# Two-layer transformer kernel: a bridge phase before the linear-attention stack, with changes to the first loads, the slot marks and the closing mixture

## What is computed

```python
def reference(...):
    # layer 0
    x = x + ga * L0_attn(layernorm(x) * (1 + ca) + sa)      # 16 heads of 64, causal, softmax
    x = x + gb * L0_ffn(layernorm(x) * (1 + cb) + sb)       # 8 experts, each takes its 512 best tokens
    # layer 1, with its own sa, ca, ga, sb, cb, gb
    x = x + ga * L1_attn(layernorm(x) * (1 + ca) + sa)      # a stack of 8 linear-attention layers
    x = x + gb * L1_ffn(layernorm(x) * (1 + cb) + sb)       # top 2 of 8 linear experts
    return x

def L0_ffn(x):          # the experts' part
    probs = softmax(rmsnorm(x) * norm_weight @ router_w.T + router_b)
    gates, idx = top_k(probs.T, 512)
    ye = gelu(xn[idx] @ fc1.T + b1) @ fc2.T + b2            # per expert
    out = zeros.at[idx].add(ye * gates);  return out / sum_of_gates_per_token

def L1_attn(x):         # 8 times
    Q = elu(x @ Wq + bq) + 1;  K = elu(x @ Wk + bk) + 1;  V = x @ Wv + bv
    att = Q * sum(K * V) / (Q * sum(K) + 1e-6)              # sums over a sequence
    x = norm(gelu(att @ Wo + bo) + x);  x = norm(gelu(gelu(x @ W1 + b1) @ W2 + b2) + x)

def L1_ffn(x):
    gates = top2(softmax(x @ Wg)), made to sum to 1
    return sum(gates[e] * (x @ We[e] + be[e]))
```

## Time and profile before

| | us |
|---|---|
| median of 3 runs | 3410.51 (3409.53 to 3415.76) |
| the profiled execution | 3412.19 |
| its span | 3410.5 |
| mean granted clock of TensorE | 0.949 |
| setup and loads | 0 to 15.9 |
| attention | 15.9 to 570 |
| router | 570 to 609 |
| choice of tokens and experts | 609 to 806 |
| combine | 806.4 to 824.4 |
| clearing of 114 semaphores | 824.4 to 832.8 |
| stack entry | 833.1 to 853.8 |
| stack up to its first matmul with weights | 854 to 874 |
| stack | 874 to 3247 |
| tail | 3247 to 3403 |
| clearing of 93 semaphores | 3403 to 3410 |

### The profile page before, as it was taken

How to read it: one execution, slowest core, us unless ns; L and a number is a source line. 1 busy time by engine, 2 the same in 40 slices (tenths; PEclk the granted TensorE clock), 3 DMA queues, 4 the chain that set the end, 5 groups by cost and what they waited for, 6 DMA issues and landing times. The chain is left out here.

```text
span 3410.5 us, 52149 instructions
## 1 busy us (share of the span) xinstructions
PE 3024.9 (89%) x14384; PEld 1972.1 (58%) x14384; DVE 2768.5 (81%) x10994; ACT 2423.9 (71%) x4513; POOL 558.3 (16%) x663
## 2 busy tenths in 40 slices
PE   6999998272599999999999999999999999999678
PEld 5777776161456565565656656656565666666342
DVE  5878786853489998988998999899899989988454
ACT  5888886031488887887887888888788888888420
POOL 0000001383101111111111111111111211211110
PEclk9999998595799999999999999999999999999869
DMA  1000000322100000000000000000000000000000
GB/s 53 1 1 1 1 0 10 103 34 36 54 1 1 5 28 2 1 7 27 1 7 26 1 3 30 2 1 7 26 1 7 26 2 2 15 1 1 0 4 22
DMA packets 35107, 46.95 MB, mean 14 GB/s; under 512 B 5704, under 2 KB 26240, under 8 KB 34816
## 3 DMA queue, kind: packets, MB, share of 16 engines
q1 hardware_dynamic: 29184, 39.47, 3.5%
q0 software_dynamic: 5632, 4.20, 0.9%
HBM read 35.16 MB, written 8.49 MB: 13 GB/s over the span
## 5 line engine op out<-in xcount | busy, mean ns | idle before, releaser
L1841 DVE TENSOR_SCALAR t_feat_q<-t_recip,t_neg_mean 128x256 f32<-128x256 f32 x1024 | 387.3, 440 | 132.7 <-ACT t_recip L1682 125.7
L1513 PE MATMUL t_o_ps<-t_feat_q,t_wo 128*128 128x512 f32 x1024 | 475.3, 597 | 13.7 <-issue 11.0
L1674 ACT ACTIVATE t_recip<-t_feat_q,t_z_scale 128x256 f32<-128x256 f32 x1024 | 434.8, 498 | 3.5 <-DVE t_feat_q L1841 2.7
L1660 ACT ACTIVATE t_exp_k<-t_k_ps 128x1024 f32<-128x1024 f32 x256 | 259.5, 1014 | 228.3 <-PE t_k_ps L1487 228.3
L1804 DVE CUSTOM_DVE_ANT_0 t_junk<-t_v_ps,t_feat_k 128x256 f32<-128x256 f32 x1024 | 390.5, 419 | 9.9 <-PE t_v_ps L1487 9.8
L1794 DVE SCALAR_TENSOR_TENSOR t_feat_k<-t_exp_k,t_k_ps 128x256 f32<-128x256 f32 x1024 | 369.0, 416 | 18.6 <-ACT t_exp_k L1660 18.5
L1664 ACT ACTIVATE t_exp_q<-t_q_ps 128x1024 f32<-128x1024 f32 x256 | 261.5, 1022 | 86.4 <-PE t_q_ps L1487 86.2
L1830 DVE SCALAR_TENSOR_TENSOR t_feat_q<-t_exp_q,t_q_ps 128x1024 f32<-128x1024 f32 x256 | 312.7, 1221 | 8.8
L1513 PEld LDWEIGHTS t_o_ps<-t_feat_q,t_wo 128*128 128x128 f32 x1024 | 194.3, 190 | 189.0 <-issue 168.9
L1972 POOL TENSOR_TENSOR t_var_eps<-t_moments,t_ln_eps 128x4 f32<-128x4 f32 x128 | 69.1, 540 | 1294.6 <-DVE t_moments L1852 1294.6
L1485 PE MATMUL t_v_ps<-t_x_hi,t_w_hi 128*128 128x512 f32 x512 | 265.3, 518 | 10.4 <-DVE t_sum_kv L1804 9.4
(11 more groups left out here) (351 smaller groups left out, 7211.4 us busy)
## 6 DMA issues: line engine op xcount, KB each, us to landing
t_raw_w<-in_wq SPq DMA_DIRECT2D x8, 512.0 KB, 4.0
t_raw_w<-in_wk SPq DMA_DIRECT2D x8, 512.0 KB, 4.6
t_raw_w<-in_wv SPq DMA_DIRECT2D x8, 512.0 KB, 6.1
t_wo<-in_wo SPq DMA_DIRECT2D x32, 128.0 KB, 2.3
x<-in_x SPq DMA_DIRECT2D x4, 512.0 KB, 7.0
tokens_dram<-r_hn SPq DMA_DIRECT2D x8, 256.0 KB, 2.3
e_w_raw<-in_fc_w SPq DMA_DIRECT2D x4, 512.0 KB, 4.0
e_w<-in_fc_w SPq DMA_DIRECT2D x4, 512.0 KB, 4.9
```

The costliest lines, as they stand in the source:

```text
L1513: last = pe.matmul(o_ps[:], wo[:, chunk, :], feat_q[:, s, chunk, :], start=(chunk == 0), stop=(chunk == NC - 1), skip_group_check=True)
L1660: act.activation(exp_k[:], k_ps[:], ACT.Exp, bias=-1.0).then_inc(c["k_exp"], 1)
L1674: last = act.activation(recip[:, q % 2, k * UNIT + n * SEQ:k * UNIT + (n + 1) * SEQ], feat_q[:, s, chunk, cols], ACT.Ln, bias=1.0, scale=z ...
L1841: last = dve.tensor_scalar(feat_q[:, s, chunk, cols], recip[:, q % 2, k * UNIT + n * SEQ:k * UNIT + (n + 1) * SEQ], -1.0, neg_mean[:, s, n ...
```

## The change

Four things are changed.

**1. First loads.** SP issues `w_q` and `w_kv` ahead of x and `w_o` behind it, in `setup_phase`. ACT rounds and DVE subtracts there too. In the attention phase SP raises `started` behind its 28 counters; the four other engines wait for it first.

The core of the diff:

```diff
 setup_phase, SP
+            sp.dma_start(g["w_raw"][:, 0, :], d["w_q"]).then_inc(g["w_in"][0], 16)
+            sp.dma_start(g["w_raw"][:, 1, :], d["w_kv"]).then_inc(g["w_in"][1], 16)
             for q in range(4):
                 sp.dma_start(g["x"][:, q * 8:q * 8 + 8, :], d["x"][:, q * 8:q * 8 + 8, :]).then_inc(x_in, 16)
+            sp.dma_start(g["w_o"][:], d["w_o"]).then_inc(g["w_o_in"], 16)
             sp.wait_ge(x_in, 64)
...
 causal_attention_phase, SP
             start_counters(sp, c.values())
-            sp.dma_start(w_raw[:, 0, :], d["w_q"]).then_inc(w_in, 16)
-            sp.dma_start(w_raw[:, 1, :], d["w_kv"]).then_inc(w_in, 16)
-            sp.dma_start(w_o[:], d["w_o"]).then_inc(w_in, 16)
-            sp.wait_ge(w_in, 48)
+            sp.sem_inc(started, 1)
+            sp.wait_ge(g["w_o_in"], 16)
...
 choose_and_run_experts_phase, ACT and DVE
+            act.activation(column_ps, column[:], ACT.Copy).then_inc(column_ready, 1)
...
-                dve.tensor_tensor(one_hot[e % 2][:], column[:].unsqueeze(1).broadcast_to([P, TILES, P]),
+                dve.tensor_tensor(one_hot[e % 2][:], column_ps.unsqueeze(1).broadcast_to([P, TILES, P]),
...
 bridge_phase, POOL
+            for k in range(TURNS + 1):
+                if k < TURNS:
+                    add_term(k)
+                if k >= 1:
+                    find_rstd(k - 1)
+                if k >= 3:
+                    split_low(2 * k - 6)
+                    split_low(2 * k - 5)
...
 bridge_phase, ACT
+            act.wait_ge(t["raw_w_in"], 49)
+            for n in range(TURNS):
+                if n < 6:
+                    round_high(2 * n)
+                    round_high(2 * n + 1)
+                modulate(n)
...
 bridge_phase, DVE
+            for k in range(TURNS + 2):
+                if k < TURNS:
+                    terms(k)
+                if 1 <= k <= TURNS:
+                    find_moments(k - 1)
+                if k >= 2:
+                    normalise(k - 2)
...
 tail_phase, POOL
+            for at in range(0, EXPERTS * TURNS, 2):
+                pool.wait_ge(c["hs_hi_ready"], at + 1)
+                if at >= RING:
+                    pool.wait_ge(c["hs_used"], at - RING + 1)
+                pool.tensor_tensor(hs_lo[:, at % RING, :], hs[:, at % RING, :], hs_hi[:, at % RING, :].bitcast(F32), ALU.subtract)\
+                    .then_inc(c["hs_lo_even"], 1)
...
 tail_phase, PE
             def expert(n, e):
                 at = EXPERTS * n + e
-                pe.wait_ge(c["hs_ready"], at + 1)
-                pe.matmul(sum_ps[n % 2][:], w_mix[:, e * D:(e + 1) * D], hs[:, at % RING, :], start=False, stop=(e == EXPERTS - 1),
+                cols = slice(e * D, (e + 1) * D)
+                pe.wait_ge(c["hs_hi_ready"], at + 1)
+                pe.matmul(sum_ps[n % 2][:], w_hi[:, cols], hs_hi[:, at % RING, :], start=False, stop=False, skip_group_check=True)
+                pe.matmul(sum_ps[n % 2][:], w_lo[:, cols], hs_hi[:, at % RING, :], start=False, stop=False, skip_group_check=True)
+                pe.wait_ge(c["hs_lo_odd"] if at % 2 else c["hs_lo_even"], at // 2 + 1)
+                pe.matmul(sum_ps[n % 2][:], w_hi[:, cols], hs_lo[:, at % RING, :], start=False, stop=(e == EXPERTS - 1),
                           skip_group_check=True).then_inc(c["hs_used"], 1)
```

More of the change, by code:

```diff
@@ L125, in _ @@
             act.activation(cond_e[:], cond[:], ACT.Exp, scale=-1.0).then_inc(exp_done, 1)
-            act.wait_ge(exp_done, 1)
+            for k in range(2):
+                act.wait_ge(g["w_in"][k], 16)
+                act.activation(g["w_hi"][:, k, :], g["w_raw"][:, k, :], ACT.Copy).then_inc(g["w_split_hi"], 1)
         @block.vector
@@ L258, in _ @@
         def _(act):
-            act.wait_ge(w_in, 48)
-            for k in range(2):
-                act.activation(w_hi[:, k, :], w_raw[:, k, :], ACT.Copy).then_inc(w_split_hi, 1)
+            act.wait_ge(started, 1)
             def drain_q(j, k):
@@ new lines, in find_moments, with normalise @@
+            def find_moments(n):
+                dve.wait_ge(c["x_added"], n + 1)
+                for i in range(GT * n, GT * n + GT):
+                    dve.bn_stats(stats[:, i, :], g["x"][:, i, :]).then_inc(c["bn_done"], 1)
+                dve.wait_ge(c["bn_done"], GT * n + GT)
+                for i in range(GT * n, GT * n + GT):
+                    dve.bn_aggr(moments[:, i, :], stats[:, i, :]).then_inc(c["stats_ready"], 1)
+            def normalise(n):
+                dve.wait_ge(c["rstd_ready"], n + 1)
+                if n >= 2:
+                    dve.wait_ge(c["x_turned"], n - 1)
+                for i in range(GT):
+                    tile = GT * n + i
+                    last = dve.tensor_scalar(xn[:, n % 2, i, :], g["x"][:, tile, :], moments[:, tile, 0:1], rstd[:, tile:tile + 1],
+                                             ALU.subtract, ALU.mult)
+                last.then_inc(c["xn_ready"], 1)
@@ L1287, in _ @@
+            for k in range(TURNS + 2):
[5 more added lines that the diff above has]
+                    normalise(k - 2)
         @block.tensor
         def _(pe):
+            pe.wait_ge(c["ones_made"], 1)
+            for q in range(QX):
+                pe.wait_ge(c["diag_ready"], 4 * q + 4)
+                pe.matmul(gate[q][:], ones[:], diag[:, 4 * q:4 * q + 4, :], start=True, stop=True).then_inc(c["gate_filled"], 1)
@@ L1689, in step @@
                     split_x(0, 0)
-                    for kind, q in SWAPS:
-                        swap(0, kind, q)
                 if Dn:
@@ L2133, in _ @@
             for n in range(TURNS):
-                if n + 1 < TURNS:
-                    copy_rows(n + 1)
-                gate_sums(n)
+                for e in range(EXPERTS):
+                    split_high(EXPERTS * n + e)
+                    if e == 0 and n + 1 < TURNS:
+                        copy_rows(n + 1)
+                    if e == 2 and n:
+                        gate_sums(n - 1)
+            gate_sums(TURNS - 1)
         @block.vector
@@ L2333, in _ @@
             LAST = EXPERTS * TURNS
-            for at in range(2):
+            pe.wait_ge(c["w_split"], 1)
+            for at in range(WIDE):
                 widen(at // EXPERTS, at % EXPERTS)
@@ L2396, in block0 @@
                 g["hn_stored"] = [sem(f"r_hn_stored{s}") for s in range(2)]
-                causal_attention_phase(nc, sem, d, g)
+                with ExitStack() as weights:
+                    held = lambda n, s, t=F32: weights.enter_context(nc.sbuf_tensor(n, s, t))
+                    g["w_raw"] = held("a_w_raw", [P, 2, CH])
+                    g["w_hi"] = held("a_w_hi", [P, 2, CH], F32R)
+                    g["w_lo"] = held("a_w_lo", [P, 2, CH], F32R)
+                    g["w_o"] = held("a_w_o", [P, NC, D])
+                    g["w_in"] = [sem(f"a_w_in{k}") for k in range(2)]
+                    g["w_o_in"], g["w_split_hi"], g["w_split_lo"] = (sem(n) for n in ("a_w_o_in", "a_w_split_hi", "a_w_split_lo"))
+                    setup_phase(nc, sem, d, g)
+                    causal_attention_phase(nc, sem, d, g)
                 g["route"] = local("route", [P, EXPERTS, TILES])
```

289 lines of the change are left out of this document (166 added, 123 removed), and 6 rows, old and new, of tables (STACK_COUNTERS, names).

## The result

The changed kernel took 3376.2 us in the median of 6 runs (3362.1 to 3388.9), the one before 3411.9 in as many. The ratio is 0.9902, 95% interval 0.988 to 0.9924, which is 33 us less. The forecast was 3367 with a range of 3352 to 3386: the time lies inside it, and above the forecast. The profiled execution took 3382.81 us, one of the slower of the six.

What follows compares the result with a forecast made beforehand. It asked which engine ends each touched phase, since each ends in a barrier: POOL in the experts, PE in the tail's loop. -7.5 - 15.5 - 12.9 + 1.4 - 8.9 = -43.4 off 3410.5 gave 3367.1, range 3352 to 3386.

Steps and rivals of the forecast that it cites:

- First loads: Kernel's start: weights loaded ahead of x and split under its load, first `bn_stats` at about 18.0, -7.5 us.
- Slot marks: Experts phase: a mark with one operand in PSUM no longer blocks POOL's gathers and scatters, -15.5 us.
- walk through the lists: Experts phase: stepping through the engines' operations in order, the phase's end comes 15.5 us earlier, last scatter about 774.
- a PSUM operand doesn't free POOL: Rival on the experts' marks: DVE work of that length blocks POOL anyway, marks gain nothing, 3383 us; chance 0.10.
- Bridge: From the combination's start to the stack's first matmul: 54.3 us against 67.2, -12.9, with 4.4 a turn, POOL the bound.
- row read for no exclusion: Bridge: POOL's 1/deviation was no longer beside DVE's normalisation, so perhaps no blocking: 38.7 us instead of 40.9.
- rival of 48 us: Bridge: moments and normalisation on DVE both exclude POOL, so its length is 48 us and the kernel 3374; chance 0.15.
- Second clearing: A later clearing clears 19 more at 73 ns each, +1.4 us.
- Tail: Tail's loop: three fp32r matmuls an expert replace one float32 matmul, -8.9 us, range -15 to +1.
- a turn of 11.1, 8 x 1.3: Tail's loop: each of eight turns takes 11.1 us instead of 12.39, giving -10.4 before other gains and costs.
- rival on the clock: Tail: gaps from the chain keep PE's clock at 0.50, a turn takes 20.3 us, kernel 3439; chance 0.06.
- the chain is late: Rival on the tail: PE waits for the rest of `hs` as often as it saves, no gain, 3376 us; chance 0.12.

Runs made afterwards that it cites:

- e11: The changed kernel once more with no edit, measured beside the kernel before: 3372.7 us, ratio 0.9877.
- e2: The changed kernel with the tail of the kernel before (one float32 matmul an expert): 3371.2 us, ratio 0.9878.
- e3: The kernel before with the new tail alone (three fp32r matmuls an expert): 3411.2 us, ratio 0.9997.
- e9: The kernel before with the reordered first loads alone: 3403.6 us, ratio 0.9965.
- e1: The kernel before with only the marks' operand `column` copied to PSUM by ACT: 3396.2 us, ratio 0.9949.
- e8: The changed kernel with POOL's twelve bridge subtractions moved behind its last 1/deviation: 3381.3 us, ratio 0.9901, bridge 38.3 us.
- e5: The changed kernel with 22 more fp32r matmuls, product unread, on PE ahead of the tail's loop: 3376.6 us, ratio 0.9887.
- e12: The changed kernel with four more fp32r matmuls, product unread, for each expert of the tail's first turn: 3370.5 us, ratio 0.9865.
- e4: The changed kernel with the float32 matmul in the first of the tail's eight turns only: 3364.9 us, ratio 0.9854.
- e7: The changed kernel with the bridge's additions of `term` to x on DVE instead of POOL: 3380.9 us, ratio 0.9898, bridge 41.9 us.

## Why the prediction was right or wrong

The number was right within its range, but as the sum of errors of both signs: in the profiled execution what stands ahead of the tail gave 4.4 us more than forecast, and the tail 18.6 less. Over all runs the new tail is worth nothing (0.9877 with it in e11 and 0.9878 with the old one in e2; e3 alone 0.9997), where -8.9 was forecast, and the larger gains ahead of it made up for most of that. That they did was luck.

1. *First loads.* Right: -8.1 for -7.5, and e9 shows it alone.
2. *Slot marks.* Right, and the reason too: e1 changes the operand and nothing else, and 17 us go. The walk through the lists put the last scatter at 774; it began at 772.38. The rival "a PSUM operand doesn't free POOL" is out.
3. *Bridge.* 3.3 us better than the sum. The term that was mis-sized is a turn of POOL: 4.4 us forecast, 3.88 measured. The forecast had the additions, 1/deviation and two subtractions at 4.0 plus 0.4 for being blocked; POOL wasn't blocked. It was DVE that was: 1.72 for 1.08 in the normalisation. The exclusion that I had let fall on POOL stretched DVE's operation instead, since POOL's addition began first (814.13 against 814.52), and hit `term` or the moments in no row (0.86 beside a subtraction). The row read for no exclusion was right for 1/deviation only: that one took 1.02 us and the normalisation 1.08 beside each other (e8), but the addition isn't like it. The estimate of 0.73 for a subtraction of 128x256, between two far bounds, was good: 0.70. The rival of 48 us is out: moments don't exclude POOL.
4. *Second clearing.* Right.
5. *Tail.* The step "a turn of 11.1, 8 x 1.3" was right at full clock and failed on its silent other half: that the clock returns as early as before ("the first five experts run at half clock ... and gain 1.5 more"). It returned after 53 us, not 9. The five are misread too: in the kernel before three experts start at half clock (3299.10, 3301.64, 3304.18). A turn takes 11.1 at full clock and 19.6 at half, so 44 us more at half clock cost 44 x (1 - 11.1/19.6) = 19.1; -8.9 + 19.1 = +10.2, measured +9.7. The rival on the clock had seen the price and mistaken the cause. It asked for gaps that PE would wait in, and there are none; and it had the clock either back or lost for good, where the length of the stretch differs from run to run. The rival "the chain is late" is out: the profile shows no wait of PE for the rest of `hs` in the loop.

What is shown: the late return belongs to the loop of fp32r matmuls (six profiles of 19 to 73 us against four of 9 with float32), it isn't the kind of number as such (e5's 22, e12), and the edits that pack the first turn closer end it (e4, e12). What isn't: whether it is the packing or the part of the small `wide` matmuls, which the same edits change, and why it is 19 us once and 73 another time with the same instructions. That the faster of the changed kernel's runs (3362 to 3371) are those of an early return is argued from their mean clock (0.949 to 0.952 for a whole run, against 0.943 to 0.947 of those above 3382), not seen in a profile.

## What to carry to other kernels

Where a change makes matmuls cheaper in a stretch that begins at half clock, cost it at both clocks, and ask whether what replaces them still brings the clock back; a first turn of closer packed matmuls can be worth more than what it costs (e4), and even matmuls whose product is thrown away cost nothing here on the whole (e12). If an operation on VectorE with two operands in SBUF stands over GpSimd's work, put the one that stays the same into PSUM: here the operation cost the same and GpSimd ran free. Work moved to GpSimd beside VectorE is paid by whichever of the two comes second (the gathers over a mark in the kernel before, VectorE's normalisation over an addition here), so look for the stretch in both.

## What the hardware showed that was not expected

- The clock stayed at 0.50 for 19 to 73 us while the profile shows PE busy at every moment. The 0.59 and 0.56 us steps between matmuls that otherwise follow in 0.43 don't show in the busy time. A full row of nines in PE's busy tenths doesn't mean a full clock; read both lines of the page.
- The Trainium skill ("SBUF — State Buffer", section "SBUF: two separate sides") lets a DVE operation with two SBUF inputs, or in two-port mode, and a GpSimd operation exclude each other. The runs agree for an addition on DVE (0.69 alone, 1.24 beside a subtraction on POOL, e7) and for the normalisation, which has one tensor (1.08 and 1.72); that it ran in the two-port mode no row shows. The moments weren't stretched, 0.86 us for four beside a subtraction, nor the normalisation beside POOL's 1/deviation (1.08, e8).
- 4.42 us is what a compare over 128x4096 takes with its broadcast operand in SBUF as bf16 and in PSUM as float32 alike.
